# A residual constant built in two halves, and new orders and banks for all engines of a four-layer graph network kernel

## The reference

```python
x = _layernorm(x + _L0_gnn_ref(x, adj, L0_gnn_W, L0_gnn_b))      # adj @ (x W + b) / row sums
x = _layernorm(x + _L1_gnn_ref(x, adj, nodemask, Wqk, Wv))       # softmax over nodes of q.(adj k), times v
x = _layernorm(x + _L2_gnn_ref(x, adj, adj, Wq, ..., bo, 128))   # 8 heads, scores times (adj + adj), softmax, Wo
x = _layernorm(x + _L3_gnn_ref(x, adj, W1, b1, gamma, beta, W2, b2))
# L3: h = layer_norm(relu(Dn * H @ (Be * H.T @ (x W1)) + b1)) * gamma + beta
#     y = Dn * H @ (Be * H.T @ (h W2)) + b2 ;  result y + x ;  H = (adj != 0)
```

## Time and profile before

| what | value |
|---|---|
| median of 3 runs | 1755.94 us (1754.32 to 1756.01) |
| the profiled execution's own time, and its span | 1754.82 us, 1753.1 us |
| busy share of the span: PE, PEld, DVE, ACT, POOL | 98%, 89%, 83%, 82%, 79% |
| granted TensorE clock | 1.000 |
| PE busy in the first 60 us, the last 58 us | 50.00 us, 48.78 us |
| mean of `y` (L1150), of statistics on 256 elements (L1026), of the aggregate (L1031) on VectorE | 0.471, 0.417, 0.176 us |
| mean of `xg` (L1064) on VectorE, of a norm of 256 elements (L724, from `x`) on ScalarE | 0.419, 0.603 us |
| GpSimd's root, from one L884 to the next (830 to 834 us) | 1.21 us |
| DMA share | 0.1 in the loop |

### The profile page before, as it was taken

One profiled execution on the slowest core, in us unless ns is written; L12 is line 12 of the kernel. 1 busy time (PEld: TensorE's weight loads), 2 busy tenths in 40 slices (PEclk: granted clock), 3 DMA queues, 4 the chain that ended last, 5 costly groups with the idle time before them and its releaser, 6 DMA issues. The chain is left out here.

```text
span 1753.1 us, 52062 instructions
## 1 busy us (share of the span) xinstructions
...
## 2 busy tenths in 40 slices
...
DMA packets 93590, 62.94 MB, mean 36 GB/s; under 512 B 8430, under 2 KB 92924, under 8 KB 93564
## 3 DMA queue, kind: packets, MB, share of 16 engines
...
q10 hardware_dynamic: 816, 1.05, 0.2%
...
## 5 line engine op out<-in xcount | busy, mean ns | idle before, releaser
L785 ACT ACTIVATE z<-z,z_max 128x128 f32<-128x128 f32 x1024 | 399.8, 398 | 5.0 <-DVE z_max L1125 3.7
L886 POOL TENSOR_TENSOR ln_rs<-ln_ve,minus_half 128x1 f32<-128x1 f32 x640 | 352.6, 551 | 50.1
L889 POOL TENSOR_SCALAR ln_nm<-ln_mv,ln_rs 128x1 f32<-128x1 f32 x640 | 170.6, 267 | 110.1 <-POOL ln_rs L886 110.0
L884 POOL TENSOR_TENSOR ln_ve<-ln_mv,eps_col 128x1 f32<-128x1 f32 x640 | 122.7, 192 | 163.1 <-DVE ln_mv L1031 162.8
L906 POOL TENSOR_TENSOR z<-z,z_rcp 128x1024 f32<-128x1024 f32 x128 | 243.1, 1899 | 8.7 <-DVE z_rcp L1132 5.5
L516 PE MATMUL ps<-w2T,mnT 128*128 128x256 f32 x1536 | 209.0, 284 | 0.0
L516 PE MATMUL ps<-w1T,txT 128*128 128x512 f32 x768 | 204.5, 403 | 0.2 <-DVE txT L1041 0.2
L785 ACT ACTIVATION_READ_ACCUMULATOR z<-z,z_max 128x1 f32 x1024 | 200.0, 195 | 0.0
L516 PEld LDWEIGHTS ps<-w2T,mnT 128*128 128x128 f32 x1536 | 188.1, 188 | 4.2 <-DVE mnT L1041 0.4
L1041 DVE TENSOR_TENSOR mnT<-ps,mnT 128x512 fp32r<-128x512 f32 x128 | 86.7, 678 | 111.5 <-ACT mnT L716 111.5
L1125 DVE TENSOR_REDUCE z_max<-z 128x4 f32<-128x512 f32 x256 | 170.2, 675 | 0.1
...
## 6 DMA issues: line engine op xcount, KB each, us to landing
x_in<-in_x_dram SPq DMA_DIRECT2D x128, 128.0 KB, 2.1
a_hold<-in_adj_dram SPq DMA_DIRECT2D x128, 128.0 KB, 2.2
out_dram<-y_out SPq DMA_DIRECT2D x128, 128.0 KB, 1.7
a_in<-in_adj_dram SPq DMA_DIRECT2D x128, 64.0 KB, 1.9
...
```

The source lines that it names most:

```text
L785: m = act.activation(z[:, g % 2, h, :], z[:, g % 2, h, :], ACT.Exp, bias=z_max[:, g % 2, h:h + 1], accum_out=z_sum[:, g % 2, h:h + 1])
L884: pool.tensor_tensor(ve[n][:, g:g + 1], mv[n][:, g, 1:2], (eps4_col if n == "ln4" else eps_col)[:, :], ALU.add).then_inc(eps_made[n], 1)
L886: pool.tensor_tensor(rs[n][:, g:g + 1], ve[n][:, g:g + 1], minus_half[:, :], ALU.pow).then_inc(root_made[n], 1)
L889: pool.tensor_scalar(nm[n][:, g:g + 1], mv[n][:, g, 0:1], rs[n][:, g:g + 1], -1.0, ALU.mult, ALU.mult).then_inc(shift_made[n], 1)
```

## The change

Three things change, and nothing in what is computed.

1. `c3_` makes the constant for two graphs at a time, so there are `c3.0` (graphs 0 and 1) and `c3.1` (graphs 2 and 3), each of two instructions on half the elements. The counts of `c3_half` and `c3_made` go by pairs, and `x3b_` waits for its own pair.
2. The order texts of all five engines are new, in all three phases. Of what the text below speaks: on GpSimd `c3.0` is followed by `x2c.3`, `x3b.0`, `wm.0`, `hb.0`, and `c3.1` stands behind the `ln1` roots; on TensorE `cx.2` and `cx.3` are neighbours, `mp.2`, `mp.3` moved from the end of the body to its beginning (of the next walk), `v2.2` from the beginning to the end, `v2.3` stays; VectorE's `z1.2` opens the body instead of standing near its end. `SP` sends the mask ahead of the first `a_in`.
3. The PSUM banks of all results are new.

The diff, with the parts for ScalarE and others cut:

```diff
@@ -18,6 +18,7 @@
 P = 128
 G = 4
 HEADS = 8
+PAIRS = G // 2
 RG = 4
 EPS = 1e-5
 TINY = 1e-37
 ORDER_TEXT = {
     "pe": """
-        cx.0:2 at.0+:4 v2.2:1 ax.0+:0 at.1+:3 at.2+:5 wo.0:7 at.3+:6 ax.1+:1 ax.2+:0 h0.0+:2 pt.1:3 h0.1+:5
-        sc1.3:6 sc0.3:1 cx.1:4 h0.2+:0 ax.3+:5 v2.3:6 tx.0:3 wo.1:2 x1t.0+:6 amx.0+:1 h0.3+:5 h1.0:0
-        x1t.1+:7 pt.2:3 amx.1+:2 xg.0+:5 x1t.2+:6 amx.2+:0 cx.2:4 xg.1+:3 amx.3+:7 x1t.3+:0 xg.2+:1 pt.3:5
-        xg.3+:4 wo.2:0 cx.3:3 tx.1:2 wt.0+:0 v1.0+:7 wo.3:3 v1.1+:6 pb.0+:5 v1.2+:4 mn.0:0 v1.3+:3 tx.2:2
-        h1.1:7 x2t.0+:6 h1.2:1 tx.3:2 x2t.1+:0 y.0:7 x2t.2+:4 x2t.3+:6 h1.3:5 q0.0+:3 k1.0+:2 q1.0+:1
-        k0.0+:5 mn.1:3 mp.0+:0 sc0.0+:1 sc1.0+:5 mn.2:7 y.1:4 mp.1+:1 mn.3:3 sc0.1+:6 sc1.1+:4 y.2:2 v2.0+:6
-        y.3:7 sc1.2+:2 sc0.2+:0 pt.0+:4 v2.1+:7 mp.2+:6 mp.3+:3
+        at.0+:4 cx.0:5 at.1+:7 mp.2:1 mp.3:2 ax.0+:0 ax.1+:3 at.2+:1 at.3+:2 wo.0:7 pt.1:4 ax.2+:1 h0.0+:0
+        sc1.3:6 sc0.3:2 cx.1:5 v2.3:0 h0.1+:6 ax.3+:1 tx.0:7 h0.2+:3 x1t.0+:0 amx.0+:6 h0.3+:1 wo.1:2 pt.2:3
+        h1.0:5 x1t.1+:7 amx.1+:0 x1t.2+:6 xg.0+:2 amx.2+:5 xg.1+:7 pt.3:1 xg.2+:4 x1t.3+:7 amx.3+:0 cx.2:5
+        cx.3:1 tx.1:6 xg.3+:2 wo.2:3 wo.3:0 wt.0+:7 h1.1:1 v1.0+:2 pb.0+:7 v1.1+:6 v1.2+:4 mn.0:0 v1.3+:2
+        tx.2:3 tx.3:6 x2t.0+:1 y.0:0 h1.2:5 x2t.1+:4 x2t.2+:3 mp.0+:7 x2t.3+:2 h1.3:0 q1.0+:2 k1.0+:1
+        k0.0+:4 q0.0+:0 mn.1:1 mp.1+:3 sc0.0+:6 sc1.0+:4 mn.2:0 v2.0+:3 sc0.1+:1 sc1.1+:6 y.1:4 mn.3:5
+        v2.1+:1 y.2:6 y.3:1 pt.0+:4 sc0.2+:2 sc1.2+:0 v2.2+:6
     """,
...
     "dve": """
-        asum.0+ cx_lo.0 zmax0.2 zmax1.2 ax_lo.0+ hT.0+ wo.0 hT.1+ hT.2+ hT.3+ ax_lo.1+ ln2_stats.0
...
-        zmax1.1+ ln4_stats.2 ln4_aggr.2 y.3 ln4_stats.3 ln4_aggr.3 z1.2+ z0.2+ zrcp.1+
+        z1.2 asum.0+ hT.0+ hT.1+ cx_lo.0 zmax0.2 ax_lo.0+ hT.2+ wo.0 ln2_stats.0 hT.3+ ax_lo.1+ ln2_aggr.0
...
+        ln4_stats.2 ln4_aggr.2 y.3 ln4_stats.3 ln4_aggr.3 zrcp.1+ z0.2+
     """,
     "pool": """
-        xb.0+ probs.1 xb.1+ xb.2+ mask.0+ dmax.0 am.0+ xb.3+ ln2_root.0 ln0_root.0+ dinv.0 ln0_root.1+
-        probs.2 ln0_root.2+ ln2_root.1 ln0_root.3+ probs.3 c3.0 wm.0+ ln3_root.0 ln2_root.2 ln2_root.3
-        ln1_root.0+ ln1_root.1+ ln1_root.2+ ln1_root.3+ x2c.0+ x2c.1+ x3b.0 hb.0+ x3b.1 ln3_root.1 x3b.2
-        ln3_root.2 x2c.2+ ln4_root.0 ln3_root.3 x3b.3 ln4_root.1 x2c.3+ probs.0+ ln4_root.2 ln4_root.3
+        xb.0+ probs.1 xb.1+ mask.0+ xb.2+ am.0+ ln2_root.0 dmax.0 ln0_root.0+ probs.2 xb.3+ ln0_root.1+
+        ln0_root.2+ dinv.0 probs.3 ln0_root.3+ ln2_root.1 c3.0 x2c.3 x3b.0 wm.0+ hb.0+ ln3_root.0 ln2_root.2
+        ln2_root.3 ln1_root.0+ ln1_root.1+ ln1_root.2+ ln1_root.3+ c3.1 ln3_root.1 ln3_root.2 ln3_root.3
+        ln4_root.0 x2c.0+ x2c.1+ x3b.1 x2c.2+ x3b.2 x3b.3 probs.0+ ln4_root.1 ln4_root.2 ln4_root.3
     """,
...
 FIRST_TEXT = {
...
     "pool": """
-        xb.0+ xb.1+ mask.0+ xb.2+ am.0+ xb.3+ ln0_root.0+ ln0_root.1+ ln0_root.2+ ln0_root.3+ rep.0+ wm.0+
-        half.0+ ln1_root.0+ ln1_root.1+ ln1_root.2+ ln1_root.3+ x2c.0+ x2c.1+ rep.1+ x2c.2+ hb.0+ x2c.3+
-        probs.0+
+        mask.0+ xb.0+ xb.1+ am.0+ xb.2+ xb.3+ ln0_root.0+ ln0_root.1+ ln0_root.2+ ln0_root.3+ rep.0+ wm.0+
+        hb.0+ half.0+ rep.1+ ln1_root.0+ ln1_root.1+ ln1_root.2+ ln1_root.3+ x2c.0+ x2c.1+ x2c.2+ probs.0+
     """,
     "sp": """
-        la.0+ lx.0+ la.1+ in_mask.0+ la.2+ la.3+ in_b0.0+ lx.1+ lx.2+ lx.3+ lh.0+ in_v.0+ lh.1+ in_vec.0+
-        lh.2+ in_k.0+ in_bias.0+ in_q.0+ in_w1.0+ in_o.0+ lh.3+ in_w2.0+
+        in_mask.0+ la.0+ lx.0+ la.1+ la.2+ la.3+ lx.1+ in_b0.0+ lx.2+ lx.3+ in_o.0+ in_v.0+ in_vec.0+
+        in_q.0+ in_w1.0+ lh.0+ lh.1+ lh.2+ in_bias.0+ in_k.0+ in_w2.0+ lh.3+
     """,
...
 LAST_TEXT = {
     "pe": """
-        cx.0:7 sc0.3:4 pt.1:2 sc1.3:0 wo.0:7 cx.1:4 v2.2:2 pt.2:5 wo.1:3 v2.3:2 cx.2:7 pt.3:1 wo.2:6 tx.0:0
-        cx.3:4 tx.1:7 wo.3:3 h1.0:1 h1.1:2 tx.2:3 tx.3:0 h1.2:4 h1.3:7 mn.0:1 mn.1:2 y.0:6 mn.2:5 y.1:3
-        mn.3:6 y.2:7 y.3:3
+        mp.2:7 mp.3:3 cx.0:2 sc0.3:6 pt.1:4 wo.0:2 sc1.3:6 v2.3:3 cx.1:5 pt.2:1 wo.1:0 cx.2:4 tx.0:1 pt.3:6
+        wo.2:3 h1.0:1 cx.3:2 tx.1:3 wo.3:4 tx.2:6 h1.1:5 h1.2:0 tx.3:5 mn.0:6 h1.3:1 y.0:7 mn.1:0 mn.2:4
+        y.1:0 mn.3:2 y.2:6 y.3:0
     """,
...
@@ -950,21 +951,23 @@
                 pool.wait_ge(dhalf_made, q + 1)
                 after(pool, read["h1"], q * G)
                 pool.tensor_tensor(d_inv[:, :], d_half[:, :], d_half[:, :], ALU.add).then_inc(dinv_made, 1)
-                after(pool, c3_half, q)
+                after(pool, c3_half, q * PAIRS)
                 pool.tensor_tensor(d_cnt[:, :], d_half[:, :], mp[:, :, P + 1], ALU.mult).then_inc(dcnt_made, 1)
 
+
             def c3_(q, g):
+                two = slice(2 * g, 2 * g + 2)
                 pool.wait_ge(dcnt_made, q + 1)
-                after(pool, x3b_made, q * G)
-                pool.tensor_tensor(c3[:, :, :], bw_all[:, :].unsqueeze(1).to_broadcast([P, G, D]),
-                                   d_cnt[:, :].unsqueeze(2).to_broadcast([P, G, D]), ALU.mult).then_inc(c3_half, 1)
-                pool.wait_ge(c3_half, q + 1)
-                pool.tensor_tensor(c3[:, :, :], c3[:, :, :], b2_all[:, :].unsqueeze(1).to_broadcast([P, G, D]), ALU.add)\
+                after(pool, x3b_made, before(q, 2 * g + 1, G))
+                pool.tensor_tensor(c3[:, two, :], bw_all[:, :].unsqueeze(1).to_broadcast([P, 2, D]),
+                                   d_cnt[:, two].unsqueeze(2).to_broadcast([P, 2, D]), ALU.mult).then_inc(c3_half, 1)
+                pool.wait_ge(c3_half, q * PAIRS + (g + 1))
+                pool.tensor_tensor(c3[:, two, :], c3[:, two, :], b2_all[:, :].unsqueeze(1).to_broadcast([P, 2, D]), ALU.add)\
                     .then_inc(c3_made, 1)
 
             def x3b_(q, g):
                 pool.wait_ge(norm_made["ln2"], nth(q, g))
-                pool.wait_ge(c3_made, q + 1)
+                pool.wait_ge(c3_made, q * PAIRS + (g // 2 + 1))
                 after(pool, norm_made["ln4"], before(q, g, G))
                 pool.tensor_tensor(x3b[:, g, :], x3[:, g, :], c3[:, g, :], ALU.add).then_inc(x3b_made, 1)
 
```

More of the change, by code:

```diff
@@ L54 @@
[L54 to L58, removed]
+        at.0+ cx.0 at.1+ mp.2 mp.3 ax.0+ v2.2 at.2+ at.3+ ax.1+ exp0.2 pt.1 ax.2+ exp1.2 ln2_norm.0 cx.1
```

93 lines of the change are left out of this document (49 added, 44 removed).

## The result

The changed kernel takes 1749.4 us (median of 6 runs, 1749.05 to 1753.49) against 1755.9 (6 runs, 1754.32 to 1756.61). The ratio is 0.997, with a 95% interval of 0.9958 to 0.9982. So it is faster, by 6.5 us and not by the 24 of the forecast, and it lies 2.4 us above the forecast's range.

A forecast was written before the change was run, and what follows sets the result against it. TensorE's queue was taken to bound the kernel; 31 x (0.40 + 0.33 + 0.11 - 0.05) = 24.5 us, less 0.45 at the start, gave 24.0 and a median of 1732 us, range 1726 to 1747.

The forecast's parts named there:

- Part 1: TensorE's `wt.0` waits for GpSimd's `wm` behind `c3.0`; halving `c3.0` removes it: 0.4 us an iteration, 12.4 us.
- Part 2: On TensorE, neighbours `cx.2` and `cx.3` save one change into tiled shape: 0.33 us an iteration, 10.2 us.
- Part 3: End of TensorE's loop body: moving `mp.2`, `mp.3` away ends a bank wait for `z1.2`: 0.11 us an iteration, 3.4 us.
- the sum: TensorE's period after the change: 53.63 - 0.40 - 0.33 - 0.11 + 0.05 = 52.84 us.
- Part 4: What becomes late next: GpSimd's ring of 52.6 us, 0.2 below TensorE's own sum; no regular wait expected.
- This ring: GpSimd `xb.0` to `ln1_root.3`, ScalarE norm, TensorE `x2t.3` to `y.3`, VectorE, GpSimd's root and branch: 52.6 us.
- The edges: First and last stages: start loses 0.45 us by the mask sent first; the new orders there 0, from -3 to +3.
- GpSimd's ring binds: Rival: ring over 0.2 us longer than summed, e.g. `c3` halves of 1.2; costs 0.2 to 0.5, 1738 to 1748; 0.20.
- The sign: Whole kernel: faster by more than about 0.2% at 0.91, same 0.03, slower 0.06.

The follow-up runs named there:

- cx_apart2: `root_slack2` with `cx.2` moved ahead of `xg.2` on TensorE, so `xg.2`, `x1t.3`, `amx.3` stand between `cx.2` and `cx.3`: 1773.5 us (1 run).
- root_slack2: `norm_later` with the previous iteration's `ln4_root.3` behind `c3.1` on GpSimd and its `ln4_norm.3` behind `relu.3` on ScalarE: 1727.7 us.
- c3_0_cut: Changed kernel, the second instruction of `c3.0` (add of b2) working on one column only, leaving out computation: 1747.6 us (1 run).
- x2c_back: Changed kernel with `x2c.3` moved on GpSimd from behind `c3.0` back to just ahead of `probs.0`: 1746.5 us.
- norm_later: `x2c_back` with `ln4_norm.3` moved in ScalarE's queue behind the first copies (`aT`, `mp`) of the next iteration: 1746.9 us.
- c3_1_cut: Changed kernel, the second instruction of `c3.1` (add of b2) working on one column only, leaving out computation: 1754.0 us (1 run).

## Why the prediction was wrong

**Part 1** was right in its mechanism and its size: the wait of `wt.0` is gone, and its worth was 0.43 (forecast 0.40). The halves measured 1.04 and 1.28 us on 128x512 instead of 1.0 and 1.2, and 2.36 us from `c3.0` to `x2c.3` instead of 2.17. There is some luck in it: `wm` ended 23.35 us after the iteration's start and not at 22.4, and was in time since `wt.0` came at 23.53 and not at 22.8; 0.2 us were left and not 0.4.

**Part 2** was right: 0.33, by the starts in `cx_apart2`.

**Part 3** was short of the gain. The pair `mp.2`, `mp.3` took 0.81 in the median at the end of the body and takes 0.45 at its new place (`root_slack2`), which frees 0.36; `v2.2` at the end takes 0.89 (856.17 to 857.06), some 0.1 more than elsewhere. So the end of the body gave 0.26 and not 0.11. What the new order saves as a whole is seen where no other ring binds: TensorE's period is 52.64 (`root_slack2`), against the 52.84 of the sum.

**Part 4** failed: "This ring is 31.5 + 0.65 + 17.5 + 2.7 + 0.26 = 52.6." From one `xb.0` to the next it took 53.45, 0.85 more. From `xb.0` (804.54) to the end of `ln1_root.3` (836.48) it was 31.9 instead of 31.5, 0.2 of the 0.4 in the half constant. To `x2t.3` it was 0.8 instead of 0.65, on to the end of `y.3` 17.4 instead of 17.5, and VectorE took 1.3 instead of 1.5 to its aggregate (855.96). Up to there the ring is longer by 0.3 only. The larger part, 0.57, is behind that: 2.03 from the aggregate to `xb.0` instead of 1.46. I let "GpSimd's root (1.2)" start as soon as `y.3`'s statistics are there. But I had read the position of `probs.0` in the new queue and not asked when it starts. It starts when `zrcp.0` does let it, at 852.17, takes 1.90, and the roots of `y.1` and `y.2` then still stand ahead of the one that I counted. So the step that failed is the wait of `probs.0`, which the sum had at nothing, and the ring that bound closes over the scores, `z`, `zrcp.0` and `probs.0`, not over `y.3`. Before the change `ln4_root.1` and `x2c.3` ran ahead of `probs.0`, at the end of an idle stretch of 3.63 us; now nothing stands there (3.26 idle), and 1.22 us more are behind it.

**What I hadn't seen at all** is that this late GpSimd stands on two more ways back to TensorE: over `ln4_norm.3`, which holds `aT` in ScalarE's queue, and over `probs.1` and `probs.2` to `pt.1` and `pt.2`. These hold 53.28 even when the first ring is cut (`c3_0_cut`, `x2c_back`, `norm_later`). With one root and its norm out of the way all of them fall together, and the period with them: 0.72 us, and 0.82 with `x2c.3` back. The gain that the changed kernel lost against the forecast's period is 31 x (53.46 - 52.84) = 19 us; the best kernel gets back 31 x (53.46 - 52.64) = 25 us by its period. By the medians it is 1749.4 - 1727.7 = 21.7, or 19.7 when each is taken against the kernel before timed beside it (-6.5 and -26.2).

**The edges**: I had a loss of 0.45 at the start and put the rest at 0, from -3 to +3. TensorE's first matmul is 0.67 later. The first stage lost 3 us to the low clock, at the end of the bounds; without it, it takes what it took (49.2 against 49.3). The last stage came out 0.4 us shorter.

**The rivals.** "GpSimd's ring binds" was the right one, at 0.20. The reason that it gave, halves of 1.2 us (they took 1.18), explains 0.2 of the 0.85; most of the rest is the queue behind `probs.0`, which it didn't name. Its price was too low: I let it cost 0.2 to 0.5 an iteration, it cost 0.6 in the profiled execution, and the first stage was dearer too. That took the time out of a range that had been drawn to hold this case. The sign, at 0.91 for faster by more than 0.2%, was right.

Open: the profiled execution of the changed kernel is 4 us slower than its other five at the same mean clock, and `c3_1_cut`'s single time is like it, so which of 53.3 and 53.46 is the usual period of the changed kernel isn't known. The best version was timed with the change's first and last stages as they are.
